# A two-layer graph network on one core: twelve dense units leave the first edge stage for the end of the program

## The reference

```python
def _L0_gnn_ref(x, edge_index, W1, b1, W2, b2):
    x_col = x[col]
    feat = jnp.concatenate([x_col, x[row] - x_col], axis=-1)
    h = jax.nn.relu(feat @ W1 + b1)
    messages = h @ W2 + b2
    out = jax.ops.segment_max(messages, col, num_segments=x.shape[0])
    return jnp.where(jnp.isneginf(out), jnp.zeros_like(out), out)
def _L1_gnn_ref(x, edge_index, W1, b1, W2, b2, Wres, bres):
    agg = jax.ops.segment_sum(x[src], dst, num_segments=x.shape[0])
    h = x + agg
    h = jnp.maximum(h @ W1 + b1, 0.0) @ W2 + b2
    return x @ Wres + bres + h
x = _layernorm(x + _L0_gnn_ref(x, edge_index, ...), axis=-1)
x = _layernorm(x + _L1_gnn_ref(x, edge_index, ...), axis=-1)
```

## Time and profile before

| | |
|---|---|
| median of three runs | 1128.31 us (1127.45 to 1129.91) |
| profiled execution, its own time | 1128.96 us |
| its span, first to last instruction | 1127.2 us |
| mean granted TensorE clock | 0.994 |
| PE busy | 1079.5 us, 96% |
| DVE busy | 935.8 us, 83% |
| ACT busy | 898.5 us, 80% |
| POOL busy | 766.1 us, 68% |

### The profile page before, as it was taken

The page is one execution under the profiler, slowest core; times in us unless marked ns, Lnnn a source line. Parts: engine busy times, 40 slices in busy tenths (PEclk is TensorE's granted clock), DMA queues, the critical chain, the costliest instruction groups (busy, mean ns, idle before and its releaser), DMA issues.

```text
span 1127.2 us, 27123 instructions
## 1 busy us (share of the span) xinstructions
PE 1079.5 (96%) x7463; PEld 832.6 (74%) x7463; DVE 935.8 (83%) x3645; ACT 898.5 (80%) x3888; POOL 766.1 (68%) x798
## 2 busy tenths in 40 slices
PE   5899999999999999999989999999999999999995
PEld 3677777776666666666668888888888878888884
DVE  7798998887888888888868787877878789999993
ACT  2888788787888888888888888888888887777775
POOL 5777777777777777761027777777777777777712
PEclk9999999999999999999999999999999999999998
DMA  5787877874777888786666767666665566666652
GB/s 147 224 247 236 242 238 234 245 222 143 222 214 222 234 222 222 216 220 180 174 216 204 209 192 215 190 211 197 199 194 166 192 193 218 219 216 217 221 174 85
DMA packets 172256, 231.86 MB, mean 206 GB/s; under 512 B 25659, under 2 KB 90792, under 8 KB 172107
## 3 DMA queue, kind: packets, MB, share of 16 engines
q1 hardware_dynamic: 145434, 180.66, 51.6%
q0 software_dynamic: 25088, 48.94, 16.8%
q10 hardware_dynamic: 1584, 0.53, 0.2%
HBM read 129.48 MB, written 102.78 MB: 206 GB/s over the span
## 4 chain that ended last, share of the span: by engine, by line
PE 60%; POOL 19%; DVE 10%; issue 8%; ACT 2%; DMA 1%; SPq 0%; DVEq 0%; POOLq 0%; ACTq 0%
POOL edge_rows L522 17%; PE psY L1125 10%; PE psY L1126 10%; PE psH L1134 9%; PE psT L1118 5%; PE psE L1118 5%; PE psE L1244 5%; DVE shared L758 4%; PE psE L1126 4%; PE psE L1125 4%; PE psE L1280 4%; DVE shared L769 2%; PE psE L1235 2%; POOL xd_early L522 1%; DVE x L609 1%
## 5 line engine op out<-in xcount | busy, mean ns | idle before, releaser
L1125 PE MATMUL psY<-wc,hT 128*128 128x128 f32 x1568 | 304.0, 276 | 0.5 <-DVE o_rows L646 0.4
L1126 PE MATMUL psY<-wcr,xT 128*128 128x128 f32 x1568 | 303.7, 275 | 0.0
L522 POOL DMA_INDIRECT edge_rows<-x1e_table,idx x196 | 188.8, 963 | 126.3 <-DMA x1e_table<-shared 66.8
L526 POOL DMA_INDIRECT out<-edge_rows,idx x196 | 195.3, 996 | 99.7 <-issue 63.1
L949 ACT ACTIVATE junk<-psY 128x128 f32<-128x128 f32 x784 | 210.1, 304 | 48.0 <-PE psY L1126 47.9
L1125 PEld LDWEIGHTS psY<-wc,hT 128*128 128x128 f32 x1568 | 238.6, 192 | 1.9 <-issue 1.9
L1126 PEld LDWEIGHTS psY<-wcr,xT 128*128 128x128 f32 x1568 | 238.7, 192 | 0.0
L522 POOL DMA_INDIRECT edge_rows<-in_x,idx x196 | 191.2, 975 | 66.1 <-issue 59.4
L609 DVE TENSOR_SCALAR x<-x_in,mv,rs 128x128 f32<-128x128 f32 x784 | 220.7, 360 | 0.6
L1134 PE MATMUL psH<-xT,wc 128*128 128x512 f32 x392 | 204.2, 603 | 6.1 <-ACT xT L944 5.6
L949 ACT ACTIVATION_READ_ACCUMULATOR junk<-psY 128x1 f32 x784 | 181.4, 235 | 0.0
(11 more groups left out here) (125 smaller groups left out, 1996.0 us busy)
## 6 DMA issues: line engine op xcount, KB each, us to landing
x_in<-in_x SPq DMA_DIRECT2D x196, 256.0 KB
out<-o_rows SPq DMA_DIRECT2D x195, 256.0 KB
src_bc<-src_dram SPq DMA_DIRECT2D x49, 256.0 KB
mask<-mask_dram SPq DMA_DIRECT2D x98, 128.0 KB
x1eT_spill<-x1eT SPq DMA_DIRECT2D x49, 256.0 KB, 2.3
x1e_table<-edge_rows SPq DMA_DIRECT2D x49, 256.0 KB, 3.2
x1e_table<-shared SPq DMA_DIRECT2D x49, 256.0 KB, 3.6
x1eT<-x1eT_spill SPq DMA_DIRECT2D x49, 256.0 KB
```

Of the source, the lines that this page charges most:

```text
L522: nc.gpsimd.indirect_dma_start(to, None, table, bass.IndirectOffsetOnAxis(idx[:, what, t:t + 1], 0)).then_inc(landed[n % FLIGHT], 16)
L526: nc.gpsimd.indirect_dma_start(table, bass.IndirectOffsetOnAxis(idx[:, SCAT, t:t + 1], 0), frm, None, bounds_check=limit, oob_is_err=False ...
L1125: t_.matmul(to[:, cut(t)], h[:, cut(t)], wc2[:, :], start=t == 0, stop=False, skip_group_check=True)
L1126: last = t_.matmul(to[:, cut(t)], xt[:, cut(t)], wcr[:, :], start=False, stop=t == TILES - 1, skip_group_check=True)
```

## The change

`A_UNITS` becomes 0. No step of the first edge stage has a dense part. `A_LAST` becomes 60, `BORDER` 63, `FIRST_B` 67 and `FIRST_C` 119, so that the drain, the border and the second edge stage take units with numbers lower by 12, and the last loop of `walk` runs over 12 more.

```diff
     HEAD = 8
     FIRST_A = HEAD + STEPS
     A_STEPS = 4
-    A_UNITS = GROUPS // A_STEPS
+    A_UNITS = 0
     A_LAST = FIRST_A + A_UNITS
     BORDER = A_LAST + STEPS - GROUPS
     FIRST_B = BORDER + SLOTS
```

## The result

The changed kernel takes 1139.96 us (median of four runs, 1139.32 to 1142.71) against 1128.87 for the kernel before on the same chip. The ratio is 1.0107, with a 95% interval of 1.0095 to 1.0119: slower by 10.7 to 13.4 us, 11.1 in the medians. The forecast was +13.0 and 1141.4 us. The profiled execution took 1140.25 us, with a span of 1138.4, 11.2 us more than that of before.

A forecast was written before the change was run, and what follows sets the result against it. The prediction took a loop over engines (5.68 us a step) to bound the first edge stage and PE the closing stage (3.09 us a unit); -24.1 + 37.1 = +13.0 us gave a 1141.4 us median, range 1137.5 to 1146.5.

The forecast's parts named there:

- The limit of the edge stage: First edge stage: a loop over engines from group to group sets a step without dense work at 5.68 us.
- The 24.1 us given back: First edge stage: 1.79 us saved in the first cycle and 22.3 us over the 44 steps after it.
- The 37.1 us at the end: Closing dense stage: 12 more units at 3.09 us each, PE's issue time, with no cover.
- The sum: Whole kernel: -24.1 + 37.1 = +13.0 us, giving 1141.4 us for the median, 1.2% slower.
- a dip of the clock at the wait for group 4: First edge stage, while PE waits for group 4's gather: an uncertain term that may cost some 2 us.
- POOL's waits: POOL's scatters waiting for output stores: waits grow by 37 us at no cost, the tail keeping its length.
- The table gathers: Behind the first edge stage: the first gather from the edge table at about 558 instead of 582 us.
- PE's busy share in the stage: First edge stage: PE about 90% busy, 5.10 of 5.68 us, at a granted clock of 1.00.
- The stage at the gathers' pace: Rival, first edge stage: without dense work the step falls to about 5.0 us, total 1111 us; chance 0.04.
- the one in which nothing is saved: Rival, first edge stage: dense work only filled gaps, the step stays at 6.19 us, total 1165 us; chance 0.04.
- a clock that falls in the stage: Rival, first edge stage: PE's idle drops the clock, some 1340 us, or 1190 in a quarter of steps; chance 0.04.
- the price of a unit in the edge stage: First edge stage: a dense unit costs 2.04 us per four-step cycle, about a third of its 3.09 us hidden.

The follow-up runs named there:

- The idle transposes: Changed kernel with four or eight idle transposes on PE added to each group step of the first edge stage: 1141.1 us with four, 1156.0 us with eight.
- the single square: Changed kernel with one square instead of four on ACT in the first edge stage's layer norm, the other three variances left at 1: 1120.6 us.
- DVE's spread: Kernel before, with DVE's scaling and statistics of the dense unit done one tile in each of four group steps: 1123.3 us, ratio 0.9962.
- longer border: Changed kernel with the twelve moved units placed between the two edge stages instead of at the end: 1143.6 us, ratio 1.0130.
- both spreads: Kernel before, with the dense unit's second product on PE and its scaling and statistics on DVE spread by tiles over the group steps: 1116.5 us, ratio 0.9894.
- PE's spread: Kernel before, with the dense unit's second product on PE spread by tiles over the group steps instead of all in the last: 1117.4 us, ratio 0.9902.

## Why the prediction was right

**The limit of the edge stage** was read from the one step without dense work, and this is the step that decided. Forecast 5.68, measured 5.66, the value that the third interval less DVE's statistics had given. The idle transposes, the single square and DVE's spread show that it is a loop over PE, ACT and DVE, and neither PE's total nor the gathers, which kept up with steps of 5.19 us in the kernel with one square.

**The 24.1 us given back.** The last scan came 25.8 us earlier, but 1.6 of these do not come from the stage's steps: the gather of group 4 landed at 285.70 instead of 287.30. POOL issued the first of these gathers at 278.93 instead of 280.98. The order of work up to the edge stage is the same in ten profiles, and in them this issue lay between 278.5 and 281.0 us and the stage's first transposes between 261.0 and 266.1, so this is how executions vary. Counted from that gather, 280.9 us became 256.8: 24.1 to 24.2 us, the forecast. Two errors cancelled in it: 44 steps were 0.02 us shorter each (-0.9), and PE waited once more, 0.7 us, for the gather of group 8.

**The 37.1 us at the end.** The last matmuls of the last second product moved from 1115.84 to 1127.13, by 11.3; with the 25.8 that is 37.1 us for 12 units, 3.09 each.

**The sum** was +13.0. In the profiles it is +11.2, and the difference is the start of the stage, 1.6 us, and roundings. The medians differ by 11.1 us, and no run takes that apart: the start of the stage is known for one execution of each kernel. The measured interval of 10.7 to 13.4 us holds both.

**One term was too small, and luck kept it out.** The prediction put a dip of the clock at the wait for group 4 at some 2 us. The changed kernel's profile had no dip there, and its wait ended at 285.70, not at 287. Three other profiles had one, and there the two intervals at this place were longer than usual by 5.5 us (longer border), 6.5 (both spreads) and 6.8 (one square), the wait itself included. Added to the measured 1140.0 us, they would have brought the time near the upper end of the range.

**Hidden terms.** POOL's waits grew by 38 us (forecast 37) and cost nothing. The table gathers began at 556.5 (forecast 558). PE's busy share in the stage was 93%, forecast about 90; by starts, 5.11 of 5.66, it is 90.

**The rivals.** The stage at the gathers' pace, the one in which nothing is saved, and a clock that falls in the stage are refuted by 5.66 us at a granted clock of 1.00. The swing of the clock that the Trainium skill (TensorE: Matmul & The Clock Gate, section on a second HAM failure mode) describes for frequent micro-idles did not come from these: PE had about 0.55 us free in every step, 0.40 of it seen as idle ahead of the first edge product, for 250 us at a granted clock of 1.00. Where the clock did fall, pieces of 1.3 us and more stood ahead of it, though not every such pair brought a fall.

**What was missed** was the other half of the comparison. The prediction took the price of a unit in the edge stage, 2.04 us, as given, and set it against 3.09. That price came in good part from the order of the work in the kernel before: spread over the steps, the same unit costs 0.98 us there. Leaving the units in the stage and spreading them gained about what moving them out lost.

## What to carry to other kernels

A stage bound by a loop over several engines can have free time on each of them, even where the profile calls PE 96% busy. Look for one step without the extra work: its length is the limit of the bare step, and what an extra unit costs is what stands above it, step by step, and not its busy time. Before moving such work out, spread it so that each step exceeds the loop as little as it can (here by 0.3 us): that was worth 1.1%, and moving it out cost 1.1%.

## What the runs showed of the hardware that was not expected

- The landing of a gather can come late. In five profiles with the same order of work before it, PE waited for the last gather of group 4, which landed between 285.7 and 288.7 us. That was 2.6 us behind its issue in the kernel before, 3.0 in the changed kernel, and 4.2, 4.5 and 4.7 with the longer border, both spreads and one square.
- In the last three of these the granted clock fell to 0.50 while PE still waited and stayed there for six to seven microseconds, and an interval of 5.2 to 5.7 us became 9.6 to 11.4.
- The same two idle gaps of PE, 1.67 and 1.32 us, were followed by a lower clock in some profiles (the kernel before, the changed kernel) and not in others (PE's spread, the longer border).
